# One kernel, three reorderings: statistics, masks behind the scores of four rounds, and the context's inverse behind the second exp

## The reference

```python
x = x + attn_stack(layernorm(x))      # four layers, below
x = x + experts(layernorm(x))         # 16 routed experts, 4 chosen a token, and a shared one

for l in range(4):
    xn = ln(h, ln1_w[l], ln1_b[l])
    q, k, v = heads of xn @ W + b     # 16 heads of 8
    scores = (q @ k.T + rel_shift((q + u) @ pos.T)) * 8 ** -0.5
    scores = where(key later than query, NEG, scores)
    h = h + softmax(scores) @ v @ Wo.T + bo
    h = h + gelu(ln(h, ln2_w[l], ln2_b[l]) @ W1.T + b1) @ W2.T + b2
```

## Time and profile before

| | |
|---|---|
| median of 3 runs | 2271.62 us (2269.3 to 2272.02) |
| profiled execution, its own time | 2270.06 us |
| its span | 2268.3 us |
| TensorE busy | 2162.1 us (95%) |
| VectorE busy | 1892.2 us (83%) |
| ScalarE busy | 1796.3 us (79%) |
| POOL busy | 1288.3 us (57%) |

### The profile page before, as it was taken

One profiled execution on the slowest core, in us unless ns is written; L12 is line 12 of the kernel. 1 busy time (PEld: TensorE's weight loads), 2 busy tenths in 40 slices (PEclk: granted clock), 3 DMA queues, 4 the chain that ended last, 5 costly groups with the idle time before them and its releaser, 6 DMA issues. The chain is left out here.

```text
span 2268.3 us, 80791 instructions
## 1 busy us (share of the span) xinstructions
PE 2162.1 (95%) x30224; PEld 1883.0 (83%) x30224; DVE 1892.2 (83%) x4659; ACT 1796.3 (79%) x2661; POOL 1288.3 (57%) x2277
## 2 busy tenths in 40 slices
PE   4899999999999999999999999999999999979999
PEld 3788888888888888888888888888888888768888
DVE  6788889888888888888888888888887888469996
ACT  2688888888888888888888888888887888845453
POOL 4556556655555555555555555555555555456764
PEclk8899999999999999999999999999999999979999
DMA  4445434434344434433344333443344334124453
GB/s 137 120 118 138 124 108 110 114 109 112 104 112 112 115 105 112 111 110 105 110 112 119 108 110 107 111 114 106 106 110 126 107 110 112 53 60 96 105 114 81
DMA packets 279136, 246.79 MB, mean 109 GB/s; under 512 B 38752, under 2 KB 269280, under 8 KB 278752
## 3 DMA queue, kind: packets, MB, share of 16 engines
q1 hardware_dynamic: 278752, 241.63, 39.5%
HBM read 31.24 MB, written 4.72 MB: 16 GB/s over the span
## 5 line engine op out<-in xcount | busy, mean ns | idle before, releaser
L987 DVE TENSOR_REDUCE rowmax<-bank 128x4 f32<-128x1024 f32 (+1 forms) x768 | 908.6, 1214 | 92.4 <-PE bank L584 89.6
L804 ACT ACTIVATE probs<-bank 128x1024 f32<-128x1024 f32 x768 | 738.2, 1024 | 127.1 <-PE bank L643 115.1
L643 PE MATMUL bank<-qstack,kstack 64*128 64x128 f32 (+1 forms) x4096 | 425.7, 301 | 14.6 <-DMA qstack<-maxrows 14.5
L584 PE MATMUL bank<-kstack,qstack 62*128 62x256 f32 (+1 forms) x4096 | 417.7, 301 | 7.0 <-DMA qstack<-base_turned 7.0
L643 PEld LDWEIGHTS bank<-qstack,kstack 64*128 64x128 f32 x4096 | 317.8, 193 | 17.5 <-DMA qstack<-maxrows 17.4
L584 PEld LDWEIGHTS bank<-kstack,qstack 62*128 62x128 f32 x4096 | 317.0, 193 | 7.5 <-issue 7.4
L1150 POOL CAST xn1T_parts<-xn1T 128x256 fp32r<-128x256 f32 x128 | 50.7, 396 | 461.3 <-ACT xn1T L812 461.3
L716 PE MATMUL bank<-w,hidden 128*128 128x128 f32 x2048 | 285.2, 283 | 3.3 <-ACT hidden L852 2.8
L606 PE MATMUL bank<-maskT_half,pick_half 64*128 64x128 bf16 (+1 forms) x3072 | 270.5, 242 | 15.1 <-ACT probs L804 5.4
L663 PE MATMUL bank<-probs,v_pad 128*32 128x256 f32 x4096 | 271.0, 382 | 0.6 <-DVE v_tok L968 0.6
L546 PE MATMUL bank<-mask_half,pick_half 64*128 64x128 bf16 (+1 forms) x3072 | 268.6, 243 | 1.7 <-ACT xn1T L812 0.7
(11 more groups left out here) (147 smaller groups left out, 5013.6 us busy)
## 6 DMA issues: line engine op xcount, KB each, us to landing
qstack<-base SPq DMA_DIRECT2D x384, 128.0 KB, 2.5
kstack<-base SPq DMA_DIRECT2D x384, 128.0 KB, 2.6
qstack<-base_turned SPq DMA_DIRECT2D x384, 128.0 KB, 2.5
turn_x<-turn_c SPq DMA_DIRECT2D x512, 32.0 KB, 1.8
ctx_den<-ctxT_raw SPq DMA_DIRECT2D x256, 64.0 KB, 2.0
ctx_num<-ctxT_raw SPq DMA_DIRECT2D x256, 64.0 KB, 2.0
factors<-rows_kept SPq DMA_DIRECT2D x64, 256.0 KB, 4.8
qstack<-maxrows SPq DMA_DIRECT2D x256, 16.0 KB
```

What stands on the lines that cost most here:

```text
L584: last = pe.matmul(bank[:, b0 + b, i * wide:(i + 1) * wide], qstack[rows, r, p0 + i, t * 128:(t + 1) * 128], kstack[rows, r, p0 + i, 0:wid ...
L643: last = pe.matmul(bank[:, b0 + b, i * wide:(i + 1) * wide], kstack[rows, r, p0 + i, kt * 128:(kt + 1) * 128], qstack[rows, r, p0 + i, q0: ...
L804: act.activation(probs[:, k], bank[:, A_BANK[k]:A_BANK[k] + 2, :], ACT.Exp, scale=SCALE).then_inc(exp_done[k], 1)
L987: dve.tensor_reduce(rowmax[:, n % 2, t, :, p0:p0 + heads], bank[:, M_BANK[k]:M_BANK[k] + 2, :].rearrange("p b (h c) -> p b h c", h=heads), ...
```

## The change

There are three edits.

1. `stats_1` moves from the head of VectorE's pass to its end, ahead of `resid_2`, and one block further on (`s + 2` for `s + 1`).
2. In four rounds the masks go behind the scores: a-side round 4, m-side round 3, m-side round 5, a-side round 3. The first scores of a bank now start it, the masks are accumulated, and the round's semaphore is raised by the last mask. The bank's waits, now in `m_bank` and `a_bank`, stand ahead of the scores. The scores of m-side round 5 also come ahead of the masks of a-side round 0 instead of behind them.
3. ScalarE's `inverse(s - 5)` moves from ahead of the exps of rounds 1, 4 and 2 to between rounds 4 and 2.

```diff
-            def m_masks(n, k):
+            def m_bank(n, k):
                 if k == 0:
                     bank_left(pe, (live(n), max_done[4], n + 1))
...
+            def m_masks(n, k):
+
+                m_bank(n, k)
                 m_mask(k, 0)
                 if k >= 2:
                     m_mask(k, 1)
 
-            def m_scores(n, k):
+            def m_scores(n, k, masks_behind=False):
...
                         last = pe.matmul(bank[:, b0 + b, i * wide:(i + 1) * wide],
                                          qstack[rows, r, p0 + i, t * 128:(t + 1) * 128],
-                                         kstack[rows, r, p0 + i, 0:wide], start=False, stop=True,
+                                         kstack[rows, r, p0 + i, 0:wide], start=(masks_behind and i == 0), stop=True,
                                          skip_group_check=True)
+                if masks_behind:
+                    m_mask(k, 0, first=False)
+                    last = m_mask(k, 1, first=False)
                 last.then_inc(scores_done[k], 1)
...
                 if live(s - 4):
-                    a_masks(s - 4, 4)
-                if live(s - 4):
-                    a_scores(s - 4, 4)
+                    a_bank(s - 4, 4)
+                    a_scores(s - 4, 4, masks_behind=True)
...
                 if live(s - 2):
-                    m_masks(s - 2, 3)
-                if live(s - 2):
-                    m_scores(s - 2, 3)
+                    m_bank(s - 2, 3)
+                    m_scores(s - 2, 3, masks_behind=True)
...
                 if live(s - 1):
-                    m_masks(s - 1, 5)
+                    m_bank(s - 1, 5)
+                    m_scores(s - 1, 5, masks_behind=True)
                 if live(s - 3):
                     a_masks(s - 3, 0)
-                if live(s - 1):
-                    m_scores(s - 1, 5)
-                if live(s - 3):
                     a_scores(s - 3, 0)
                 if live(s - 3):
-                    a_masks(s - 3, 3)
-                if live(s - 3):
-                    a_scores(s - 3, 3)
+                    a_bank(s - 3, 3)
+                    a_scores(s - 3, 3, masks_behind=True)
...
-                if live(s - 5):
-                    inverse(s - 5)
                 if live(s - 4):
                     exp_round(s - 4, 1)
                 if live(s - 4):
                     exp_round(s - 4, 4)
+                if live(s - 5):
+                    inverse(s - 5)
                 if live(s - 4):
                     exp_round(s - 4, 2)
...
+            stats_1(0)
             for s in SLOTS:
-                if live(s + 1):
-                    stats_1(s + 1)
...
                 if live(s - 2):
                     maxrows_out(s - 2)
+                if live(s + 2):
+                    stats_1(s + 2)
                 if live(s - 6):
                     resid_2(s - 6)
```

More of the change, by code:

```diff
@@ L537, in values, with m_mask @@
                 last.then_inc(v_done, 1)
-            def m_mask(k, half):
+            def m_mask(k, half, first=True):
                 heads = 4 if k < 2 else 2
@@ L545, in m_mask @@
                     c = (0 if k < 2 else 128) + half * 64
-                    pe.matmul(v[:, :, c:c + 64], pick_half[rows, half], mask_half[rows, half, 0:heads],
-                              start=(half == 0), stop=True, skip_group_check=True)
-            def m_masks(n, k):
+                    last = pe.matmul(v[:, :, c:c + 64], pick_half[rows, half], mask_half[rows, half, 0:heads],
+                                     start=(first and half == 0), stop=True, skip_group_check=True)
+                return last
+            def m_bank(n, k):
                 if k == 0:
@@ L597, in m1, with a_mask @@
                 last.then_inc(max_turned, 1)
-            def a_mask(k, half):
+            def a_mask(k, half, first=True):
                 heads = 2 if k % 3 < 2 else 4
@@ L605, in a_mask, with a_bank @@
                     c = half * 64
-                    pe.matmul(v[:, :, c:c + 64], pick_half[rows, 2 + half], maskT_half[rows, half, 0:heads],
-                              start=(half == 0), stop=True, skip_group_check=True)
-            def a_masks(n, k):
+                    last = pe.matmul(v[:, :, c:c + 64], pick_half[rows, 2 + half], maskT_half[rows, half, 0:heads],
+                                     start=(first and half == 0), stop=True, skip_group_check=True)
+                return last
+            def a_bank(n, k):
                 if k == 0:
@@ L625, in a_masks @@
                     bank_left(pe, (live(n + 3), cosines_used, n + 4), (live(n - 3), xn2T_ready, n - 2))
+            def a_masks(n, k):
+                a_bank(n, k)
                 a_mask(k, 0)
@@ L628, in a_masks, with a_scores @@
                     a_mask(k, 1)
-            def a_scores(n, k):
+            def a_scores(n, k, masks_behind=False):
                 r, b0 = n % RING, A_BANK[k]
@@ L644, in a_scores @@
                                          kstack[rows, r, p0 + i, kt * 128:(kt + 1) * 128],
-                                         qstack[rows, r, p0 + i, q0:S], start=False, stop=True,
+                                         qstack[rows, r, p0 + i, q0:S], start=(masks_behind and i == 0), stop=True,
                                          skip_group_check=True)
+                if masks_behind:
+                    a_mask(k, 0, first=False)
+                    last = a_mask(k, 1, first=False)
                 last.then_inc(scoresT_done[k], 1)
```

## The result

The changed kernel takes 2356.6 us (2351.6 to 2359.9, four runs) against 2270.7 us. The ratio is 1.038, between 1.037 and 1.040 at 95%. So it is slower, as forecast, but by 86 us instead of 56, and 7 us above the range.

A forecast was written before the change was run, and what follows sets the result against it. The loop through POOL, SyncE, TensorE and ScalarE bounds it: 2.83 + 7.21 to 7.34 + 5.41, taken as 15.50 us; 123 x 15.50 + 14 is +61, cut to +55, so 2327 us, range 2290 to 2350.

The forecast's parts named there:

- the loop: POOL's L1190, query turn, SyncE's DMAs, round 5 scores, next first exp: forecast to set the pass at 15.50 us.
- The slack of 0.77 us: Between L1190 and the round 5 scores: L1190 could be 0.77 (or 0.64) us later without lengthening the pass.
- the held passes: Two passes before the change where POOL's weight splits delayed L1190; scores followed it by 7.21 and 7.34 us.
- nothing comes back before the next exp: From round 5 scores to the next first exp: 5.41 us in a delayed pass as in an even one.
- The even pass: The usual pass: forecast to grow from 14.89 to 15.50 us, from sums of 15.45 to 15.58.
- Rival 1: Scores to exp: the 0.22 us wait inside the 5.41 goes, giving a 15.28 us pass and 2300 us; 15%.
- uneven passes: Passes longer than the even one: 28 us in all before the change, forecast to fall to 14 us.
- The 6 us that the forecast took off at the end: Lowered +61 to +55: 1 or 2 us in the last four passes, up to 4 for a sooner round 5.
- Rival 2: Turn path: f32 weight loads show behind waits, or `maxrows` lands late more often; 0.1 to 0.3 us a pass; 13%.
- The masks: Masks behind scores in four blocks on TensorE: taken as 0 us a pass, between +0.4 and -0.2.
- The statistics: VectorE's moved statistics remove TensorE's wait before L128: 0.22 us a pass if TensorE's loop sets the end, otherwise 0.
- Rival 4: No change: uneven passes offset even ones, or passes of 14.9 to 15.0 with `values` behind the third exp; 2271 us; 4%.

The follow-up runs named there:

- the filler kernels: Kernel before with one or two spare powers on POOL ahead of L1190, other engines unchanged: 2306.1 us with one, 2380.0 us with two.
- one filler of 0.68: Kernel before with one spare power on POOL ahead of L1190, delaying its product by 0.68 us: 2306.1 us, ratio 1.015.
- edit 3 alone: Kernel before with only ScalarE's inverse moved behind the second exp: 2366.0 us, ratio 1.042.
- the turn free: Changed kernel with SyncE's maxima DMAs ahead of the turned queries: 2293.7 us, shortest pass 15.08; with the inverse also back: 2246.9 us, commonest pass 14.77.

## Why the prediction missed its size

**The mechanism was right, step by step.** L1190 starts 2.77 us behind the first exp (forecast 2.83), ScalarE is its releaser, `maxrows` releases the scores in each pass, the waits for L987 went, and the filler kernels show the loop without ScalarE. The slack of 0.77 us read from the held passes was right: one filler of 0.68 left the shortest passes as they were, two put them at the forecast 15.5. That nothing comes back before the next exp was right but for 0.11 us, which edits 1 and 2 gave (5.30 for 5.41; edit 3 alone has 5.41).

**The even pass** was forecast at 15.50 and is 15.28, 123 x 0.22 = 27 us too slow in all. Of the 0.22, 0.11 is that stretch, 0.06 is L1202's start, and 0.05 lay between 15.50 and the forecast's own lowest sum, 15.45. Rival 1's pass of 15.28 is the measured one, but only half of its 0.22 came, and the rest of the agreement is luck.

**The step that failed is "uneven passes".** The prediction took 28 us of uneven passes from the mean before, subtracted what the longer pass would cover, and left 14 us. Measured after are 123 x (15.81 - 15.27) = 66 us. The whole sum, then: forecast +61 for the 123 passes, less 27 for the even pass, and 52 more for the uneven ones, is the measured +86. The 6 us that the forecast took off at the end didn't come either (the rest of the span is 1.3 us longer). The error of the even pass hid half of the error of the uneven ones, so the forecast of +55 was nearer than its terms.

Some 39 of the 52 us lie between L1190 and the scores (48 us of spread after, 10 before, each taken above its lowest tenth and summed over the 119 passes). They have two parts of like size, and the prediction priced neither. First, it counted the delays that had shown in the passes before, and not those that the 0.77 us of slack had been hiding. By the same measure the landing of the maxima behind L1190 had 28 us of spread before, of which 10 showed in the scores: some 19 us were hidden and could have been read from the trace before. Second, after, the landing has 48. The other 20 are new, and they are in the three turned-query issues (9 us before, 38 after; the landing has less than before). The change moved these issues to where in the pass SyncE's issues are often stretched, and why they are stretched there stays open. The last 13 of the 52 us are not allotted: the delays ahead of L1190 that the forecast took off did fall, from 12 us to 3, but the passes show no such gain in all.

Rival 2, at 2340 to 2360 and 13%, holds the measured time. Of its two reasons, the load behind a wait didn't show (scores to exp became shorter). That `maxrows` is late more often with no slack to hide it is what happened, but the landing itself was not slower: it was the issues ahead of it.

**The masks** were taken at 0 between +0.4 and -0.2: alone they cost 0.07 us a pass (14.97 against 14.90). That is near the 0.10 by which the f32 load is longer than the bf16 one, and one such wait is in the trace (L656, above), but no run shows that the load is the reason. The Trainium skill's rule for a load, weighed there ("TensorE: Matmul & The Clock Gate", section LDWEIGHTS), gave 0.01.

**The statistics** were said to be worth 0.22 us a pass if TensorE's own loop set the end. Alone they give 14.90 - 14.71 = 0.19.

**The next loop.** Rival 4's loop by the third exp was put at 15.0 and is 15.08. It makes the third edit a loss even with the turn free: 14.77 against 15.08, as said above.

## What to carry to other kernels

Follow what stands *behind* the waiting instruction, on its own engine and on the next: the inverse ended some 1.7 us before its reader began, and what paid was the unrelated work queued behind that reader on POOL and, behind that, on SyncE. A pass held up by something rare is a free experiment on the slack of its loop; look for one before you price a delay. And slack that seems spare in the commonest pass may be in use in the others: when a change eats it, add the spread of the segments that it covered, and don't carry over the uneven passes of before. Even that spread is a lower estimate here, since the change also moved three issues to a place in the pass where they are late more often.

## What the runs showed of the hardware

The issue of a DMA on SyncE takes about 0.6 us, but 7% of them take 1.3 to 1.4 in the mean and up to 2.2. In the changed kernel 125 of the 136 that take more than 0.8 us begin within 0.45 us behind, or 0.10 ahead of, the start of a packet of instructions on queue q8. In this kernel's passes an issue of the turned queries that starts 11.4 to 11.8 us behind the scores of round 5 is stretched in a fifth to a quarter of the passes (20 to 26 of about 95, in six kernels), and one that starts before 11 us in at most 8 of 100. With these issues on the path, the pass pays for it according to where they fall. The cause is not isolated.
